# One block of programs for a decoder layer: shared FFN chunks in the attention's last steps, a denser rank chain, twelve shared groups in routing

## What is computed

```python
x = layernorm(x + attn(x, Wq, bq, Wk, bk, Wv, bv))   # q: softmax over features; k, v: over tokens
x = layernorm(x + xattn(x, ctx, ctx))                # (q ctx^T) ctx, linear, no softmax
x = layernorm(x + ffn(x, ...))

def ffn(h):
    probs = softmax(flat @ gate_W.T)                 # 8 experts
    top_v, top_i = top_k(probs, 2)
    g = silu(einsum('td,edf->etf', flat, w1_e)); u = einsum('td,edf->etf', flat, w3_e)
    out_e = einsum('etf,efd->etd', g * u, w2_e)      # F = 512
    routed = einsum('te,etd->td', gates, out_e)
    gs = silu(einsum('bsd,ndf->nbsf', h, w1_s)); us = einsum('bsd,ndf->nbsf', h, w3_s)
    shared = einsum('nbsf,nfd->bsd', gs * us, w2_s) / 8
    return 0.5 * shared + 0.5 * routed
```

## Time and profile before

| | us |
|---|---|
| median of 3 runs | 832.73 |
| lowest, highest | 830.67, 832.78 |
| the profiled execution | 838.74 |
| its span | 836.6 |
| mean granted TensorE clock | 0.936 of full |

### The profile page before, as it was taken

One profiled execution on the slowest core, in us unless ns is written; L12 is line 12 of the kernel. 1 busy time (PEld: TensorE's weight loads), 2 busy tenths in 40 slices (PEclk: granted clock), 3 DMA queues, 4 the chain that ended last, 5 costly groups with the idle time before them and its releaser, 6 DMA issues.

```text
span 836.6 us, 16313 instructions
## 1 busy us (share of the span) xinstructions
PE 708.8 (85%) x5111; PEld 645.5 (77%) x5112; DVE 481.3 (58%) x1434; ACT 479.3 (57%) x1440; POOL 466.1 (56%) x471
## 2 busy tenths in 40 slices
PE   5889999874999998888889888889888898999930
PEld 3667888763788888888878887888788887998830
DVE  2799999954899853333343333343343333546996
ACT  4889999922399722445444444444444444644786
POOL 3378988862111165666666666666676666441322
PEclk8899999975899998999999999998999999999975
DMA  5457555623211241111111111111111112125583
GB/s 173 152 175 229 163 183 171 164 75 101 76 52 51 58 129 35 45 45 44 43 42 42 49 42 42 42 46 41 45 42 46 42 45 43 29 62 160 145 221 101
DMA packets 87266, 72.98 MB, mean 87 GB/s; under 512 B 10066, under 2 KB 72410, under 8 KB 87194
## 3 DMA queue, kind: packets, MB, share of 16 engines
q1 hardware_dynamic: 77808, 53.43, 21.6%
q0 software_dynamic: 9088, 18.63, 8.2%
q10 hardware_dynamic: 298, 0.01, 0.0%
HBM read 50.14 MB, written 21.89 MB: 86 GB/s over the span
## 4 chain that ended last, share of the span: by engine, by line
PE 56%; issue 8%; DVE 7%; ACT 3%; POOL 1%; DMA 0%; POOLq 0%; ACTq 0%
PE bank L1333 15%; PE bank L1297 10%; PE bank L1299 9%; PE bank L1298 9%; PE bank L1003 3%; PE bank L1289 2%; ACT oh_code L1052 2%; PE bank L992 2%; PE bank L993 1%; PE bank L994 1%; DVE xg L1626 1%; DVE oh_blk L1123 1%; PE bank L1540 1%; DVE f_st L1643 1%; PE bank L1528 1%
## 5 line engine op out<-in xcount | busy, mean ns | idle before, releaser
L1416 DVE TENSOR_TENSOR s_hT<-s_sg,bank 128x512 f32<-128x512 f32 x142 | 97.5, 687 | 256.5 <-PE bank L1299 127.7
L1297 PE MATMUL bank<-e_x_hi,e_w_hi 128*128 128x256 f32 x568 | 175.3, 309 | 35.4 <-issue 34.9
L1256 POOL DMA_INDIRECT y_rows<-e_y,dst_tab x142 | 148.7, 1047 | 90.3 <-ACT e_y L1365 54.6
L1248 POOL DMA_INDIRECT xg<-x_rows,src_tab x142 | 145.2, 1023 | 67.1 <-issue 30.6
L1299 PE MATMUL bank<-e_x_hi,e_w_lo 128*128 128x256 f32 x568 | 164.5, 290 | 9.8 <-issue 9.6
L1298 PE MATMUL bank<-e_x_lo,e_w_hi 128*128 128x256 f32 x568 | 163.6, 288 | 3.5 <-issue 3.4
L1359 ACT ACTIVATE s_sg<-bank 128x512 f32<-128x512 f32 x142 | 84.8, 597 | 140.6 <-remote 89.5
L1297 PEld LDWEIGHTS bank<-e_x_hi,e_w_hi 128*128 128x128 f32 x568 | 110.8, 195 | 45.7 <-issue 44.2
L1333 PE MATMUL bank<-w,s_hT 128*128 x1136 | 140.5, 278 | 0.1
L1333 PEld LDWEIGHTS bank<-w,s_hT 128*128 128x128 f32 x1136 | 134.8, 194 | 1.5 <-issue 1.3
L1299 PEld LDWEIGHTS bank<-e_x_hi,e_w_lo 128*128 128x128 f32 x568 | 111.0, 195 | 10.5 <-issue 10.2
(11 more groups left out here) (167 smaller groups left out, 1522.8 us busy)
## 6 DMA issues: line engine op xcount, KB each, us to landing
yk<-y_rows SPq DMA_DIRECT2D x16, 512.0 KB, 4.4
xT_in<-in_xT_dram SPq DMA_DIRECT2D x16, 256.0 KB, 3.2
x_res<-in_x_dram SPq DMA_DIRECT2D x16, 256.0 KB, 3.7
w_in<-in_L_ffn_w_e_dram SPq DMA_DIRECT2D x16, 256.0 KB, 3.0
c_in<-in_ctx_dram SPq DMA_DIRECT2D x16, 256.0 KB, 2.9
cT_in<-in_ctxT_dram SPq DMA_DIRECT2D x16, 256.0 KB, 3.1
x_rows<-x SPq DMA_DIRECT2D x16, 256.0 KB, 2.4
x2T_cols<-x2T SPq DMA_DIRECT2D x16, 256.0 KB, 2.7
```

The costliest lines, as they stand in the source:

```text
L1248: nc.gpsimd.indirect_dma_start(xg[b % XR][:, t, :], None, x2_rows, bass.IndirectOffsetOnAxis(src_tab[:, i:i + 1], 0)).then_inc(gathered[b ...
L1256: nc.gpsimd.indirect_dma_start(y_rows, bass.IndirectOffsetOnAxis(dst_tab[:, n:n + 1], 0), y[b % R][:, t, :], None).then_inc(scattered[b % ...
L1297: nc.tensor.matmul(at, w_hi[r % 2][:, w], x_hi[r][:, :], start=True, stop=False)
L1416: nc.vector.tensor_tensor(hT[par][:, half * HC:(half + 1) * HC, :].rearrange("p c n -> p (c n)"), sg[half][:, :], bank[2 + half][:, :], AL ...
```

## The change

1. All four stages' programs stand in one block; nothing joins the engines after the attention. The buffers of the shared FFN (`Common`) are allocated beside those of the attention. `x2_all`, which lies over the attention's buffers, is loaded once the last logits are done.
2. The shared FFN's weights are loaded first instead of last (`expert_of`).
3. The first `PRE = 6` chunks stand in the attention's steps 18 to 20, between their remaining matmuls. Group 14's transposition and logits use bank 5 instead of 7, and group 15's transposition waits for the top places of group 13.
4. `ranks` stands in chunk 6, and the six parts of `place_of` stand two behind each of the chunks 6, 7 and 8. `C0` is 9 instead of 8, `table_at` 33.
5. `EARLY` is 12: 48 chunks before the experts, 16 in combine. POOL issues 30 gathers before the experts' first block instead of 16, and 104 instead of 118 after those and the eight of the first blocks. The x_lo of the groups 9, 10 and 11 stand between gathers (`between`).
6. The exponential of the gates on ACT moves from the stage's start to behind chunk 32, between two silus; the program gets a table load before it and one after it.

```diff
-EARLY = 10
+EARLY = 12
+PRE = 6
-    OC, C0 = 6, 2 * FC
+    OC, C0 = 6, PRE + 3
+    LATER = (LOOK + 2 - 2) // FC + 2
...
                 @block.tensor
                 def _(pe):
                     ahead, run = one.tensor(pe)
-                    zero.tensor(pe, ahead)
+                    early, rest = zero.tensor(pe, ahead)
+                    first.tensor(pe, early)
+                    rest()
                     run()
...
+    def logit_bank(g):
+        return 5 if isinstance(g, int) and g == NG - 2 else 7
...
             def turn_x2(g, gj, gp):
                 pe.wait_ge(xn_ok[1], g + 1)
-                if later(g, 1):
+            if isinstance(g, int) and g == NG - 2:
+                pe.wait_ge(sx_ok, NG)
+            elif isinstance(g, int) and g == NG - 1:
+                pe.wait_ge(ix_ok, NG - 2)
+            elif later(g, 1):
                     pe.wait_ge(ix_ok, g)
```

TensorE's last attention steps (`early(n)` is chunk n):

```diff
+            if i == NG + 2:
+                logits(*at(6))
+                turn_x1(*at(3))
+                turn_x2(*at(5))
...
+                early(0)
+                cross_scores(*at(3))
...
+                cross_mix(*at(3))
+                early(1)
+            if i == NG + 3:
+                logits(*at(6))
+                turn_x2(*at(5))
+                early(2)
+                early(3)
```

VectorE's, where `early(n)` is the product of chunk n and `top` stands for the three top-two operations:

```diff
+            if i == NG + 3:
+                spread(1, *at(4))
+                early(0)
+                early(1)
+                top(*at(TOP))
+            if i == NG + 4:
+                top(*at(TOP))
+                early(2)
+                early(3)
+            if i == NG + 5:
+                early(4)
+                top(*at(TOP))
```

GpSimd (ahead of a chunk's gathers), ScalarE and VectorE in routing:

```diff
+        def between(n):
+            g = (n - 2) // FC + 1
+            if (n - 2) % FC == 0 and LATER <= g < EARLY:
+                x_low(g)
...
+                if n == LOOK + 1:
+                    act.wait_ge(exp_in, 1)
+                    nc.scalar.activation(e8[:, :, :], e8[:, :, :], ACT.Exp).then_inc(exp_ok, 1)
...
-        for n in range(EARLY * FC):
+            for n in range(PRE - 1, EARLY * FC):
...
-            if n < C0:
-                place_of(n)
+                if PRE <= n < C0:
+                    place_of(2 * (n - PRE))
+                    place_of(2 * (n - PRE) + 1)
```

1288 lines of the change are left out of this document (699 added, 589 removed).

## The result

| us | before | after |
|---|---|---|
| median of 4 runs | 831.70 | 811.34 |
| lowest, highest | 830.26, 832.78 | 807.79, 812.28 |
| profiled execution, its span | 838.74, 836.6 | 811.53, 809.7 |
| mean granted TensorE clock | 0.936 | 0.956 |

The ratio is 0.9761, with a 95% interval of 0.9732 to 0.9791: 20.4 us faster. 829.8 was forecast, with a range from 815 to 841. The profiled executions differ by 27; that of before lies 7 above its median, that of after at its median.

The account below looks back on a forecast made before the run. It took TensorE as nearly full except at the attention's end and the combine, with VectorE also full in the one-hot parts. -5.9 + 16.0 + 2.9 - 8.5 - 7.4 = -2.9 from 832.7 gave 829.8 us, range 815 to 841.

Parts of the forecast that it names:

- A: End of the attention and rank chain: product of the first chunk with a one-hot part comes earlier, -5.9 us.
- B: Before the experts: seven more chunks at 2.285 us each, hidden by nothing, +16.0 us.
- C: GpSimd's order before the experts: x_lo of groups 10 and 11 come late behind gathers, +2.9 us.
- D: Experts: 14 more gathers issued before the weight casts begin, each saving 0.61 us, -8.5 us.
- E: Combine: eight chunks fewer, a group without chunks takes 2.98 us, -7.4 us.
- law G: Not in the prediction, read from the result: GpSimd's chain of indirect DMAs is the bound from first to last gather.
- rival 2: Experts: GpSimd's load per block is a threshold, -15 to -25 us there, 818.3 in all; chance 0.18.
- Rival 3: Attention's tail: the clock stays half, -0.5 instead of -5.9 us, 835.1 in all; chance 0.10 together with rival 4.
- rival 4: Attention's end: filled steps delay the last top places to 210, -1.6 us there, 834.1; chance 0.10 together with Rival 3.
- Rival 1: Experts: gathers cost the same wherever they stand, so moving them saves nothing; 838.3 us in all; chance 0.24.
- Rival 5: Combine: bound by the DMAs, -4 us there, 833.2 in all; chance 0.06.

Follow-up runs that it names:

- a_one: Changed kernel with every second of the 104 gathers in the experts left out; 767.83 us, beside 830.22 for the kernel before.
- a_onescatter: Changed kernel with one scatter for an expert block instead of two, all gathers kept; 763.81 us, beside 836.93 for the kernel before.
- a_nocast: Changed kernel with VectorE's copy of the experts' low weights cut from 1024 to 8 columns from block 2 on; 817.28 us, kernel before 830.22.
- c_early10: Changed kernel with EARLY = 10 instead of 12; 825.85 us, beside 836.93 for the kernel before.
- a_again: The changed kernel itself, run again in a later set; 825.69 us, beside 836.93 for the kernel before.
- a_xlo10: Changed kernel with EARLY = 10 and group 9's x_lo computed by VectorE instead of GpSimd; 814.52 us, beside 830.48 for the kernel before.
- a_xlo: Changed kernel with the x_lo of groups 9, 10 and 11 computed by VectorE instead of GpSimd; 812.13 us, beside 830.48 for the kernel before.
- d_two10: Changed kernel with EARLY = 10, two one-hot parts per chunk, first 30 gathers over 18 chunks, late x_lo on VectorE; 755.92 us, kernel before 759.60.

## Why the prediction was wrong, point by point

By the forecast's own terms, from the rows above, the 26.9 us between the spans are: A -9.6 and one-hot parts +1.1 (forecast -5.9); from the last one-hot part to the first down product 43.4 before and 57.7 after, +14.4 (B and C, forecast +18.9); from there to the last down pass -24.7 (D, forecast -8.5); to the end -8.0 (E, forecast -7.4). **The step that failed is D**, with 16 of the 24 us that the forecast is off between the traces.

**D, forecast -8.5, measured -24.7** (416.5 to 391.7; up to 7 of that is the slow profiled execution of before). The forecast divided a loss of 83.8 us by 138 gathers and took 0.61 us as the price of each, 14 x 0.61. The division was the error: under a limit there is no loss at all (a_one, a_onescatter), so the loss cannot be shared out. Above it, law G would have a DMA cost its whole 1.54 us, 14 x 1.54 = 21.6. That is near the timed pair, but the pairs within a set gave 0.7 and 1.1 us a gather, so the price above the limit stays open between 0.7 and 1.8. The reason given for it, the weight cast, was an onset in time (304.20) taken for a cause; a_nocast and the late product at 300.71 speak against it. By the forecast's own signs the mean block fell from 6.10 to 5.7 us, the value that it had given to rival 2.

**A, forecast -5.9, measured -9.6.** The mechanism held. From the count to the product behind the first one-hot part it took 13.46 us, forecast 13.6. The mis-sized piece is the last top places: 202.94 for 205.7. The full clock was let begin at 189; the cross scores at 184.40 already took 1.34 us in place of 2.05, and each later step of the row came earlier in turn. Rival 3 (half clock) and rival 4 (late top places) did not occur; the working of rival 3 gives +0.1 for A (five times 1.2), not -0.5. One small thing was missed: the one-hot stage takes 1.1 us longer.

**B, forecast +16.0, and C, +2.9.** Sizes right, 15.0 and 3.2 where no signal is late. In the timed pair the two took 14.4. But the reason "Nothing hides them, PE is full" does not reach past the first gathers. It was read from chunks 30 to 36, ahead of most gathers; behind them TensorE has time to fill, 1.22 us in each expert block. How much of the added chunks it hides depends on the set: eight chunks fewer shorten the stretch from first to last gather by 11.6 us (c_early10 and a_again) or by 2.9 (a_xlo10 and a_xlo).

**Rival 2 was nearest the truth** with a threshold in GpSimd's DMAs per block and 818.3; it set the threshold by 1.28 us a DMA. What was held against it ("blocks take 6.10, not 5.0, so GpSimd has idle time") was the misreading: 6.10 / 3.9 is 1.56, within the 1.51 to 1.59 of every kernel of that kind above the limit, and the idle time is time in which GpSimd waits for a late signal. The range gave it half a size. **Rival 1** (a moved gather saves nothing) did not occur in the sets of 830 to 837. In the quick kind it came near: -9.6 + 1.1 + 15.0 + 3.2 - 8.0 is +1.7, and -3.2 was measured, which leaves some 5 us for the blocks in place of 25.

**E, forecast -7.4, measured -7.38** between the same groups, -8.0 to the end. Rival 5 fell: with groups 2.98 us apart the DMAs kept up.

How far off the forecast is depends on the set too: the changed kernel gained 2.4% when it was timed, 1.3% beside a_onescatter and 0.5% beside d_two10. No run shows which of these is to be expected next time.

## What to carry to other kernels

When an engine that is off the critical path issues DMAs nearly without a break, divide the stretch by their number, in several stages or versions. A quotient that stays near one value while the other engines' work changes says that the number of DMAs sets the pace, even if the engine shows waits and is busy for only 68 of 100 us. Then work added to the other engines in that stretch costs little, and what counts is when the chain starts and how many links it has. Look at how far the quotient scatters before you forecast with it: here its spread was as large as the gain. And a loss should not be divided by a count before one knows that it falls in proportion; half the count would have told it.
